# A read of shifted positions that also waits for the head two further on

## The chip, the cores and the metric

The kernel runs on one core of a Trainium2 chip. The metric is the device time of one execution in microseconds, the median of several runs.

## What is computed

The reference normalises x (32 sequences of 512 tokens, 256 wide) and adds to x an attention with relative positions and a mixture of experts. Only the attention matters here. For each of 32 x 16 heads:

```python
content_score = jnp.einsum('bhsp,bhtp->bhst', q + u, k)
pos_score = jnp.einsum('bhsp,htp->bhst', q + v, pos)
pos_score = _relative_shift(pos_score)
score = (content_score + pos_score) / jnp.sqrt(jnp.float32(P))
weights = jax.nn.softmax(score, axis=-1)
out = jnp.einsum('bhst,bhtp->bhsp', weights, val)
```

`_relative_shift` puts a zero column before a 512 x 512 matrix, reads the same memory as rows of 512, and drops the first one. It is a pure change of addresses.

## The kernel before

**Stages.** A first stage (up to about 180 us) normalises x, stores it and computes the gate. The attention follows, up to about 3,360 us, one head after the other: 16 iterations of 32 heads (two sequences). Iterations 0 to 2 and 15 are written out, iterations 3 to 14 are one hardware loop. The experts follow.

**One head through the engines.** The body of every engine counts steps `kk` of 0 to 31, and one step is one head long. Head n (counted over all iterations) goes through these places:

- TensorE computes its position scores (L978) in step n-5, in four quarters.
- ScalarE copies them out of PSUM in two halves (`x_evacuate`, L605) into `ring`, with a zero column in front. The second half ends at the end of step n-5 and brings the semaphore `x_out` to 2(n+1).
- SyncE waits for that and writes the head to memory (`write_x`, L397), 1,026 KB, into one of 8 slots of `xs_d`.
- GpSimd waits until this write has landed (`x_written`), and until the slot of `shifted` that it will fill is free (`t_full`, head n-8), and reads the head back (`read_x`, L497), 1,024 KB, one row further on. That is the relative shift. In the order of GpSimd's program the read of head n stands at the beginning of step n-3.
- VectorE adds the shifted positions to the content scores (`add`, L745), first quarter at the end of step n-1. This is the first use of what was read, and the first quarter waits for the read (`x_shifted`).
- ScalarE takes the exponential (L610), TensorE transposes (L1011), and VectorE and ScalarE copy that out (L755, L619). TensorE multiplies with the values (L1027).

Reads and writes of heads are thus long transfers of about 1 MB, on two queues: q1 (SyncE) and q0 (GpSimd).

**What else stands in GpSimd's program.** GpSimd splits operands into a high and a low part, in the order of its own program:

```python
for kk in range(BH):
    t = kk // MH + 1
    if not (last and kk + LEAD - 2 >= BH):
        read_x(i, kk + LEAD - 2)
    if kk % MH == 4 and not (last and t >= TILES):
        keys(i, t)
    if kk % MH == 5 and not (last and t >= TILES):
        with_u(i, t)
    if kk % MH == 6 and t % 2 and not last:
        split_xt(i * 2 + 2 + t // 2, t // 2)
    if kk % MH == MH - 1 and not (last and t + 1 >= TILES):
        with_v(i, t + 1)
```

Here `MH` is 8 (heads in one tile of queries), `LEAD` is 5. `with_u` and `with_v` are a CAST (L457) and a TENSOR_TENSOR (L459) each. `with_u` reads `qn[:, 0]` and `with_v` reads `qn[:, 1]`. `keys` is L477 and L479, `split_xt` is L487 and L489.

**Who waits for these.** Once in 8 heads, ScalarE writes the next tile of queries into `qn` (`keep_queries`, two ACTIVATEs, L569). It overwrites what `with_u`, `with_v` and `keys` read, so it waits for all three of the tile before (`qu_low`, `qv_low`, `k_low`). It stands in ScalarE's step `kk % 8 == 6`, behind the first two exponentials, and ahead of the first half of `x_evacuate` (L605) of that step. TensorE waits for it (`q_kept`), because the projection and `spread_kd` (L900, L902) use one PSUM bank in turn, and then goes on with the scores of the same step. The `with_u` whose result frees `qn[:, 0]` stands in GpSimd's step `kk % 8 == 5`, directly behind the read of head kk+3.

**Boundary of the loop.** At the start of each turn of the hardware loop TensorE and ScalarE pause for new instructions. Step 0 is then 12 to 17 us long instead of 5 to 7.

Of the kernel before, what the change touches and what calls it, by code (L numbers as in the profile page):

```python
# [41 lines left out]
def wait(eng, sem, value):  # L42

    if isinstance(value, int) and value <= 0:
        return
    eng.wait_ge(sem, value)


def wait_alone(eng, sem, value):

    wait(eng, sem, value)
    if not isinstance(value, int):
        eng.nop(nofuse=True)
# [92 lines left out]
def attention_phase(nc, x, gate_w, w, w1, w2, consts, xn_d, xt_d, xs_d, att_d, sums_d, shared):  # L146
# [5 lines left out]
    EARLY = 3  # L152
    LEAD = 5
    LAG = 2
    NX = 8
    NW = 4
    BH = 2 * H
# [5 lines left out]
    ITERS = B // 2  # L163
    with ExitStack() as ctx:
# [11 lines left out]
        pos = m.sb("pos", [P, NG8, S], F32R)  # L176
        shifted = m.sb("shifted", [P, NX, TT, S])

# [18 lines left out]
        xo = shared.ring[:, :].rearrange("p (k t c) -> p k t c", k=NW, t=TT)  # L197
        mn = m.sb("mn", [P, NX, TT])
        pt = m.sb("pt", [P, TT, S])
# [89 lines left out]
        x_out = m.sem("x_out")  # L289
        x_written = [m.sem(f"x_written{k}") for k in range(NX)]  # L290
        x_shifted = [m.sem(f"x_shifted{k}") for k in range(NX)]
        s_full = m.sem("s_full")
# [25 lines left out]
        def values_at(kk, last):  # L318

            half = {9: 0, H - 1: 1}.get(kk % H)  # L320
            return (kk // H + 1, half) if half is not None and not (last and kk // H + 1 >= 2) else None
# [9 lines left out]
        def of_slot(kk):  # L331

            return kk % NX, kk // NX

# [4 lines left out]
        with nc.Block() as block:  # L339

            @block.sync
            def _(sp):
# [48 lines left out]
                def write_x(i, kk):  # L391
# [3 lines left out]

                    wait_alone(sp, x_shifted[slot], (i * (BH // NX) + turn) * 16)
                    sp.dma_start(xs_d[slot].rearrange("(p t c) -> p t c", t=TT, c=S + 1), xo[:, kk % NW]).then_inc(x_written[slot], 16)  # L397
# [43 lines left out]
            def _(pool):  # L441
# [49 lines left out]
                def read_x(i, kk):  # L491

                    slot, turn = of_slot(kk)
                    wait_alone(pool, x_written[slot], (i * (BH // NX) + turn + 1) * 16)

                    wait_alone(pool, t_full, (i * BH + kk - NX + 1) * TT)
                    pool.dma_start(shifted[:, slot], xs_d[slot][S:S + S * S].rearrange("(p t c) -> p t c", t=TT, c=S)).then_inc(x_shifted[slot], 16)  # L497
# [7 lines left out]
                pool.wait_ge(p_low, DC)  # L505
                pool.wait_ge(w_low, 1)
                read_x(0, 0)
                for n in range(NS):
                    pool.wait_ge(xn_stored[n], 16 * (B // NS))
                    pool.wait_ge(xt_stored[n], 16 * (B // NS))  # L510
                read_x(0, 1)
                read_x(0, 2)
                with_v(0, 1)
                split_xt(1, 1)
# [27 lines left out]
            def _(act):  # L542
# [56 lines left out]
                def x_evacuate(i, kk, half):  # L599

                    if half == 0 and not (isinstance(i, int) and i * BH + kk < NW):
                        slot, turn = of_slot(kk - NW)
                        act.wait_ge(x_written[slot], (i * (BH // NX) + turn + 1) * 16)
                    act.wait_ge(x_full, (i * BH + kk) * 2 + half + 1)
                    act.activation(xo[:, kk % NW, 2 * half:2 * half + 2, 1:S + 1], xp[:, :, :], ACT.Copy).then_inc(x_out, 1)  # L605

                def exponential(i, kk, t):

                    act.wait_ge(added, (i * BH + kk) * TT + t + 1)
                    act.activation(shifted[:, kk % NX, t], shifted[:, kk % NX, t], ACT.Exp, bias=mn[:, kk % NX, t:t + 1],  # L610
                                   scale=-1.0).then_inc(exp_done, 1)

                def t_evacuate(i, kk):

                    n = i * BH + kk
                    act.wait_ge(t_full, (n + 1) * TT)

                    wait(act, o_full, n)
                    act.activation(pt[:, TT - 1], tp[:, 1], ACT.Copy).then_inc(t_out_act, 1)  # L619

                def o_evacuate(i, q):
                    u = i * QUADS + q
                    act.wait_ge(o_full, (u + 1) * QH)

                    wait(act, o_stored[q % 2], (u - q % 2) * (TT * 16))
                    act.activation(osb[:, q % 2].rearrange("p h t -> p (h t)"), op[:, :], ACT.Copy).then_inc(o_out, 1)
# [15 lines left out]
                def body(i):  # L642
                    first = isinstance(i, int) and i == 0
                    last = isinstance(i, int) and i == ITERS - 1
                    for kk in range(BH):
# [15 lines left out]
                        if positions:  # L661
                            x_evacuate(i, kk + LEAD, 1)
                        if not (first and kk < LAG):
                            t_evacuate(i, kk - LAG)
                        if kk % QH == 2 and not (first and kk < QH):
# [3 lines left out]
                for t in range(1, TT):  # L669
                    exponential(ITERS, -1, t)  # L670
                for k in range(LAG):
                    t_evacuate(ITERS, k - LAG)
                o_evacuate(ITERS - 1, QUADS - 1)

            @block.vector
            def _(dve):
# [61 lines left out]
                def add(i, kk, t):  # L738

                    n = i * BH + kk  # L740
                    if t == 0:
                        slot, turn = of_slot(kk)
                        wait_alone(dve, x_shifted[slot], (i * (BH // NX) + turn + 1) * 16)
                    wait_alone(dve, s_full, n * TT + t + 1)
                    dve.tensor_tensor_reduce(out=shifted[:, kk % NX, t], in0=sp_[:, t % 2], in1=shifted[:, kk % NX, t], scale=-0.25,  # L745
                                             scalar=-NEG, op0=ALU.add, op1=ALU.min,
                                             accum_out=mn[:, kk % NX, t:t + 1]).then_inc(added, 1)

                def t_evacuate(i, kk, t):
                    n = i * BH + kk  # L750
                    dve.wait_ge(t_full, n * TT + t + 1)
                    if t == 0:

                        wait(dve, o_full, n)
                    dve.tensor_copy(pt[:, t], tp[:, t % 2]).then_inc(t_out_dve, 1)  # L755
# [74 lines left out]
                def body(i):  # L830
                    first = isinstance(i, int) and i == 0
                    last = isinstance(i, int) and i == ITERS - 1
                    for kk in range(BH):
                        even, odd = even_group(kk, last), odd_group(kk, last)
                        values = values_at(kk, last)
                        turning = not (first and kk < LAG)
                        add(i, kk, 1)
                        add(i, kk, 2)
                        if turning:
                            t_evacuate(i, kk - LAG, 0)  # L840
                            t_evacuate(i, kk - LAG, 1)
# [738 lines left out]
def build(nc, x, Wq, bq, Wk, bk, Wv, bv, Wp, bp, Wo, bo, u, v, gate_w, w1, w2, out):  # L1580
    names = ("sinusoid", "ident", "first_row", "spread")
    c = {n: nc.inline_tensor(a, name=f"const_{n}").ap() for n, a in zip(names, shape_constants())}
    xn_d = nc.dram_tensor("xn_d", [B * S, D], F32).ap()
    xt_d = nc.dram_tensor("xt_d", [B, P, DC, S], F32).ap()
    ffn_d = nc.dram_tensor("ffn_d", [B * S, D], F32).ap()
    xs_d = nc.dram_tensor("xs_d", [S * P + 8 * S * (S + 1)], F32).ap()[S * P:].rearrange("(k n) -> k n", k=8)
    att_d = nc.dram_tensor("att_d", [B, D, S], F32).ap()
    sums_d = nc.dram_tensor("sums_d", [B, H, S], F32).ap()
    inv_d = nc.dram_tensor("inv_d", [B, H, S], F32).ap()
    mid_d = nc.dram_tensor("mid_d", [B, S, D], F32).ap()  # L1590
    weights = {"Wq": Wq, "Wk": Wk, "Wv": Wv, "Wp": Wp, "bq": bq, "bk": bk, "bv": bv, "bp": bp,
               "u": u.rearrange("a h b p -> (a h b p)"), "v": v.rearrange("a h b p -> (a h b p)")}
    with ExitStack() as ctx:
        shared = Shared(nc, ctx)
        attention_phase(nc, x, gate_w, weights, w1, w2, (c["sinusoid"], c["ident"], c["first_row"], c["spread"]), xn_d, xt_d, xs_d,
                        att_d, sums_d, shared)
        ffn_phase(nc, x, Wo, bo, w1, w2, xn_d, shared, ffn_d, att_d, sums_d, inv_d, mid_d, out)
# [27 lines left out]
```

## Time and profile before

| | us |
|---|---|
| median of 3 runs (range) | 5040.58 (5020.95 to 5041.53) |
| the profiled execution | 5030.14 |
| its span, first to last instruction | 5028.3 |
| TensorE busy | 4825.9 (96%) |
| VectorE busy | 3691.6 |
| ScalarE busy | 3462.9 |
| GpSimd busy | 1711.7 |
| mean granted clock of TensorE | 0.98 |

Times in the rows are microseconds from the start of the span, unless marked ns. PE is TensorE's matmul, PEld its weight load, DVE VectorE, ACT ScalarE, POOL GpSimd and SPq SyncE, which only issues transfers. L497 is a line of the kernel. A row of the timeline has start, duration, engine, line, operation, what is written and read, how many were merged, and in brackets how long the engine sat idle before it and what ended that. Where several semaphores were waited for, the bracket names the last event that the profile could find; it can name an engine that had long been done.

### The profile page before, as it was taken

Reading aid. Unit: us, or ns where it says so; the run is one execution under the profiler, and the core shown is the slowest. Engines: PE = TensorE matmul, PEld = TensorE weight load, DVE = VectorE, ACT = ScalarE, POOL = GpSimd, SP = SyncE. Lnnn points to the kernel's source line nnn. Section 1 sums busy time; section 2 is a strip of 40 time slices with the busy share of each in tenths; the row PEclk is TensorE's granted clock in tenths of the full one; section 3 lists DMA queues with packets and bytes.
Section 4 is the critical chain, followed back from the end, with each engine's and each line's share of the span. In section 5 each row is a group of like instructions: output and inputs, shape, how many; then the busy total and the mean of one; then the engine's idle time right before and its main releaser. Section 6 shows DMA issues by size and latency. Waiting matters only on the chain. (4 is left out here: it accounts for less than half of the span.)

```text
span 5028.3 us, 126515 instructions
## 1 busy us (share of the span) xinstructions
PE 4825.9 (96%) x42412; PEld 3683.7 (73%) x42412; DVE 3691.6 (73%) x8040; ACT 3462.9 (69%) x5180; POOL 1711.7 (34%) x1545
## 2 busy tenths in 40 slices
PE   7899999999999999999999999989999999999997
PEld 3566666676676666766666667758999898998997
DVE  7799998898898888988888889874455545444344
ACT  3688888898888888988978889864433333344454
POOL 1122222232223222322222222224566565544443
PEclk9899999999999999999999999999999999999999
DMA  9899999999999999999999999986445455433359
GB/s 351 318 361 347 332 360 342 351 361 337 366 349 345 362 335 346 366 343 359 359 328 360 339 344 366 366 296 179 100 115 141 113 133 140 109 62 68 60 146 312
DMA packets 320461, 1391.16 MB, mean 277 GB/s; under 512 B 42912, under 2 KB 120608, under 8 KB 188448
## 3 DMA queue, kind: packets, MB, share of 16 engines
q1 hardware_dynamic: 196896, 778.35, 41.7%
q0 software_dynamic: 122880, 604.05, 39.3%
q8 instruction: 385, 6.31, 0.5%
q14 instruction: 300, 2.46, 0.1%
HBM read 708.00 MB, written 674.23 MB: 275 GB/s over the span
## 5 line engine op out<-in xcount | busy, mean ns | idle before, releaser
L745 DVE CUSTOM_DVE_ANT_0 att_shifted<-att_quad,att_shifted 128x512 f32<-128x512 f32 x2048 | 1327.1, 684 | 213.2 <-PE att_quad L990 170.5
L610 ACT ACTIVATE att_shifted<-att_shifted,att_mn 128x512 f32<-128x512 f32 x2048 | 1361.9, 717 | 122.0 <-issue 100.4
L605 ACT ACTIVATE ring<-att_quad 128x1024 f32<-128x1024 f32 x1024 | 1047.1, 1023 | 310.8 <-PE att_quad L978 309.5
L1011 PE MATMUL att_tp<-ident,att_shifted 128*128 128x128 f32 x8192 | 1134.4, 282 | 7.1 <-issue 4.4
L755 DVE COPY att_pt<-att_tp 128x512 f32<-128x512 f32 x1536 | 1011.8, 686 | 141.2 <-PE att_tp L1011 124.0
L1011 PEld LDWEIGHTS att_tp<-ident,att_shifted 128*128 128x128 f32 x8192 | 886.8, 142 | 308.3 <-issue 145.4
L497 POOL DMA_DIRECT2D att_shifted<-xs_d x512 | 279.3, 545 | 2249.7 <-DMA xs_d<-ring 1259.3
L1482 DVE TENSOR_TENSOR ffn_hp<-ring,ffn_hp 128x512 fp32r<-128x512 f32 x512 | 474.6, 927 | 683.8 <-ACT ring L1419 638.3
L1417 ACT ACTIVATE ffn_hp<-ffn_up 128x512 fp32r<-128x512 f32 x512 | 306.0, 598 | 920.5 <-PE ffn_up L1563 864.8
L978 PE MATMUL att_quad<-att_pos,att_qv 64*128 64x512 f32 x2048 | 848.1, 454 | 38.3 <-ACT ring L605 38.2
L990 PE MATMUL att_quad<-att_kd,att_qu 64*128 64x512 f32 x2048 | 787.0, 456 | 68.9 <-issue 50.0
L1524 PE MATMUL ffn_yp<-ffn_w2p,ffn_hp 128*128 128x256 f32 x6144 | 827.7, 284 | 4.0 <-DVE ffn_hp L1482 2.3
L1524 PEld LDWEIGHTS ffn_yp<-ffn_w2p,ffn_hp 128*128 128x128 f32 x6144 | 798.7, 191 | 41.7 <-DVE ffn_hp L1482 2.7
L1563 PE MATMUL ffn_up<-ffn_xp,ffn_w1p 128*128 128x512 f32 x3072 | 795.8, 394 | 6.7 <-DVE ffn_xp L1442 2.8
L1357 POOL DMA_INDIRECT ffn_d<-ring,picks x256 | 431.1, 1684 | 702.2 <-DVE ring L1450 688.9
L990 PEld LDWEIGHTS att_quad<-att_kd,att_qu 64*128 64x128 f32 x2048 | 318.9, 187 | 438.4 <-issue 304.8
L1563 PEld LDWEIGHTS ffn_up<-ffn_xp,ffn_w1p 128*128 128x128 f32 x3072 | 546.4, 190 | 98.1 <-issue 4.5
L1027 PE MATMUL att_op<-att_pt,att_val 128*17 128x128 f32 x16384 | 559.3, 278 | 7.1 <-issue 0.2
L1027 PEld LDWEIGHTS att_op<-att_pt,att_val 128*17 128x17 f32 x16384 | 409.7, 98 | 199.5 <-issue 149.9
L978 PEld LDWEIGHTS att_quad<-att_pos,att_qv 64*128 64x128 f32 x2048 | 351.6, 188 | 71.3 <-ACT ring L605 41.4
L619 ACT ACTIVATE att_pt<-att_tp 128x512 f32<-128x512 f32 x512 | 306.2, 598 | 30.3 <-PE att_tp L1011 27.6
L1419 ACT ACTIVATE ring<-ffn_up 128x512 f32<-128x512 f32 x512 | 303.9, 593 | 8.1 <-DVE ffn_hp L1482 7.5
(111 smaller groups left out, 4707.7 us busy)
## 6 DMA issues: line engine op xcount, KB each, us to landing
xs_d<-ring SPq DMA_DIRECT2D x512, 1026.0 KB, 9.4
att_shifted<-xs_d POOLq DMA_DIRECT2D x512, 1024.0 KB, 9.9
att_shifted<-in_L_attn_x_dram SPq DMA_DIRECT2D x32, 512.0 KB, 7.2
xn_d<-att_shifted SPq DMA_DIRECT2D x32, 512.0 KB, 6.5
xt_d<-att_shifted SPq DMA_DIRECT2D x32, 512.0 KB, 7.6
gathered<-xt_d SPq DMA_DIRECT2D x32, 512.0 KB, 11.6
att_d<-att_osb SPq DMA_DIRECT2D x512, 32.0 KB
ring<-in_L_ffn_w_dram SPq DMA_DIRECT2D x16, 1024.0 KB
```

What stands on the lines that cost most here:

```text
L605: act.activation(xo[:, kk % NW, 2 * half:2 * half + 2, 1:S + 1], xp[:, :, :], ACT.Copy).then_inc(x_out, 1)
L610: act.activation(shifted[:, kk % NX, t], shifted[:, kk % NX, t], ACT.Exp, bias=mn[:, kk % NX, t:t + 1], scale=-1.0).then_inc(exp_done, 1)
L745: dve.tensor_tensor_reduce(out=shifted[:, kk % NX, t], in0=sp_[:, t % 2], in1=shifted[:, kk % NX, t], scale=-0.25, scalar=-NEG, op0=ALU.ad ...
L755: dve.tensor_copy(pt[:, t], tp[:, t % 2]).then_inc(t_out_dve, 1)
L978: ins = pe.matmul(xp[:, t % 2, :], qv[rows, kk // GH % 2, t * P:(t + 1) * P], pos[rows, kk // GH % NG8, :], start=True, stop=True)
L990: pe.matmul(sp_[:, t % 2, :], qu[rows, kk // GH % 2, t * P:(t + 1) * P], kd[rows, kk // GH % 2, :], start=True, stop=True).then_inc(s_full, 1)
L1011: ins = pe.transpose(tp[:, c % 2, t * P:(t + 1) * P], shifted[:, kk % NX, t, c * P:(c + 1) * P], ident[:, :])
L1027: ins = pe.matmul(op[32 * t:32 * t + HD + 1, kk % QH * P:(kk % QH + 1) * P], val[:, kk // H % 2, c, kk % H, :], pt[:, c, t * P:(t + 1) * P ...
L1357: pool.indirect_dma_start(ffn_d, bass.IndirectOffsetOnAxis(ap=picks[:, g * GB + k, e:e + 1], axis=0), ys[:, g % 2, k], None, compute_op=AL ...
L1482: dve.tensor_tensor(hp[:, g % 2, 1, f], hf[:, f % 2], hp[:, g % 2, 0, f].bitcast(F32), ALU.subtract).then_inc(h_low, 1)
L1524: ins = pe.matmul(yp[:, k % 2, 0:D], hp[:, g % 2, hi, f, k * CAP:(k + 1) * CAP], w2p[:, wi, f, :], start=(f == 0 and s == 0), stop=(f == F ...
L1563: ins = pe.matmul(up[:, f % 4, :], w1p[:, wi, c, f * P:(f + 1) * P], xp[:, g % 2, xi, c, :], start=(s == 0 and c == 0), stop=(s == 2 and c ...
```

## The change

`read_x` on GpSimd gets one more wait. Beside its own write's landing, the read of head n waits until `x_out` shows that head n+2 has been copied out of PSUM. This is the very count for which SyncE waits before it issues the write of head n+2. In the last iteration the head waited for is capped at the last one.

```diff
     LAG = 2
+    BESIDE = 2
     NX = 8
...
                     wait_alone(pool, x_written[slot], (i * (BH // NX) + turn + 1) * 16)
+                    final = isinstance(i, int) and i == ITERS - 1
+                    with_write = min(kk + BESIDE, BH - 1) if final else kk + BESIDE
+                    wait_alone(pool, x_out, (i * BH + with_write + 1) * 2)
 
                     wait_alone(pool, t_full, (i * BH + kk - NX + 1) * TT)
```

`wait_alone` is a wait, and behind it a nop of its own where the value is a register's (in the hardware loop). No transfer and no computation is added or removed.

## Rows read from the trace of the kernel before

**Rows 1.** The page: busy time of each engine over the span.
```profile
PE 4825.9 (96%) x42412; PEld 3683.7 (73%) x42412; DVE 3691.6 (73%) x8040; ACT 3462.9 (69%) x5180; POOL 1711.7 (34%) x1545
```

**Rows 2.** Stretches: from:to, length, busy of the engines, clock, DMA share, GB/s.
```profile
1400.00:1800.00 400.00, 383.38 (x3949) 269.52 (x3950) 340.77 (x805) 340.58 (x487) 106.88 (x120) 0.97 0.97 349
...
1783.00:1799.00 16.00, 16.00 (x133) 10.93 (x134) 11.68 (x28) 12.34 (x19) 0.53 (x1) 0.80 0.58 229
...
1862.00:1869.00 7.00, 7.00 (x69) 5.03 (x69) 5.56 (x14) 6.48 (x10) 2.83 (x3) 1.00 0.99 390
```

**Rows 3.** Timeline, step 14 of one loop turn: with_u done early.
```profile
1861.02 0.57 POOL L497 DMA_DIRECT2D att_shifted<-xs_d  x1 [1.37 <-PE att_tp L1011]
...
1862.18 1.02 ACT L605 ACTIVATE ring<-att_quad 128x1024 f32<-128x1024 f32 x1 [0.56 <-PE att_quad L978]
...
1862.80 0.69 DVE L745 CUSTOM_DVE_ANT_0 att_shifted<-att_quad,att_shifted 128x512 f32<-128x512 f32 x1
1862.86 1.55 POOL L459 TENSOR_TENSOR att_qc<-att_qn,att_qc 128x512 fp32r<-128x512 f32 x1
...
1863.33 6.79 SPq L397 DMA_DIRECT2D xs_d<-ring  x2
...
1864.92 1.25 ACT L569 ACTIVATE att_qn<-att_mp,att_bias_q 128x512 f32<-128x512 f32 x2
...
1867.00 0.48 PE L900 MATMUL att_mp<-att_kc,att_spread 128*128 128x512 f32 x1
...
1869.26 0.69 DVE L745 CUSTOM_DVE_ANT_0 att_shifted<-att_quad,att_shifted 128x512 f32<-128x512 f32 x1
...
1874.91 0.69 DVE L745 CUSTOM_DVE_ANT_0 att_shifted<-att_quad,att_shifted 128x512 f32<-128x512 f32 x1
```

**Rows 4.** Timeline, step 22 of a later turn: with_u done late.
```profile
2705.30 1.02 ACT L605 ACTIVATE ring<-att_quad 128x1024 f32<-128x1024 f32 x1 [0.56 <-PE att_quad L978]
...
2705.91 0.69 DVE L745 CUSTOM_DVE_ANT_0 att_shifted<-att_quad,att_shifted 128x512 f32<-128x512 f32 x1
2706.10 0.57 POOL L497 DMA_DIRECT2D att_shifted<-xs_d  x1 [4.54 <-PE att_tp L1011]
...
2707.92 1.56 POOL L459 TENSOR_TENSOR att_qc<-att_qn,att_qc 128x512 fp32r<-128x512 f32 x1
...
2709.56 1.26 ACT L569 ACTIVATE att_qn<-att_mp,att_bias_q 128x512 f32<-128x512 f32 x2 [1.42 <-issue]
...
2710.88 0.50 PE L900 MATMUL att_mp<-att_kc,att_spread 128*128 128x512 f32 x1 [0.51 <-ACT att_qn L569]
...
2712.96 0.69 DVE L745 CUSTOM_DVE_ANT_0 att_shifted<-att_quad,att_shifted 128x512 f32<-128x512 f32 x1
...
2719.06 0.69 DVE L745 CUSTOM_DVE_ANT_0 att_shifted<-att_quad,att_shifted 128x512 f32<-128x512 f32 x1
```

**Rows 5.** L569 (keep_queries): its count, and what its engine idled for before.
```profile
L569 ACT ACTIVATE att_qn<-att_mp,att_bias_q x128: 672/681/692, 107.6 to 3251.0; 128x512 f32<-128x512 f32 x128
...
  issue: 16.0, 24
```

**Rows 6.** Issues of the two transfers: count, KB, median us to landing.
```profile
xs_d<-ring SPq DMA_DIRECT2D x512, 1026.0 KB, 9.4
att_shifted<-xs_d POOLq DMA_DIRECT2D x512, 1024.0 KB, 9.9
```

**Rows 7.** Waits over the span: who for whom, us in total, times, longest.
```profile
POOL att_shifted L497 <- DMA xs_d<-ring: 1259.3, 268, 31.9
...
DVE att_shifted L745 <- DMA att_shifted<-xs_d: 24.8, 23, 2.8
```

**Rows 8.** Timeline: TensorE's first matmul after the pause at a loop turn.
```profile
1775.01 0.79 PE L990 MATMUL att_quad<-att_kd,att_qu 64*128 64x512 f32 x1 [4.79 <-issue]
```

**Rows 9.** Timeline: copy-out of head 278, first add of head 276.
```profile
1886.34 1.02 ACT L605 ACTIVATE ring<-att_quad 128x1024 f32<-128x1024 f32 x1 [0.56 <-PE att_quad L978]
...
1897.88 0.69 DVE L745 CUSTOM_DVE_ANT_0 att_shifted<-att_quad,att_shifted 128x512 f32<-128x512 f32 x1
```

## The prediction

> **What bounds the kernel now.** I read the page first. TensorE is busy for 96% of the span [rows 1], and in a plain stretch of the attention for 383 of 400 us [rows 2]. So whatever makes TensorE wait in the attention is paid, and little else is. In the same stretch the DMA engines show a share of 0.97 and 349 GB/s, and 390 GB/s in a dense seven microseconds [rows 2]. They are close to a limit too. The list of waits then tells how often the transfers decide: VectorE waited only 24.8 us, 23 times, for a shifted head [rows 7]. The reads have slack at nearly every head.
>
> Then I went to the timeline, for two questions. When is the read of head n issued now, against the copy-out of head n+2? And what stands behind it on GpSimd? In the ordinary case the copy-out of the second half (L605) ends at 1862.18 + 1.02 = 1863.20 and the read had been issued at 1861.02, 2.18 us earlier [rows 3]. It follows its own write's landing [rows 7], and a write takes 9.4 us while two steps take 11 to 13 [rows 6, 3]. So in most steps the new wait ends last, and the read moves later.
>
> **Part 1, the direct one: the read comes later.** Nothing is added to the transfers. The read is now issued at the end of the copy-out of head n+2 plus some 0.2 us. SyncE, which waits for the same count, issued at 1863.33, 0.13 us behind the end [rows 3]; GpSimd has one more wait and a nop to pass, so I take 0.2 (0.1 to 0.4 as bounds). What is left until its first use? The shortest case [rows 9]: the copy-out of head 278 ends at 1887.36 and the first add of head 276 starts at 1897.88, which is 10.52 us. With 0.2 for the issue and about as much again for the wake of VectorE, the read must land within about 10.1 us. Its median is 9.9 [rows 6]. In the timeline 6 of 32 steps have a window this short; the others have 11.6 us or more. Six heads in 16 iterations are 96 reads, half of them over the median. If these are late by 0.5 us on average, that is 24 us of new waits.
>
> Against it stands the 24.8 us of old waits [rows 7]. They occur when the DMA engines are behind, at 390 GB/s. Part 2 below lengthens every eighth step by 1.5 us, 3% of some 50 us, so the same bytes ask for about 339 GB/s instead of 349. I expect over half of the old waits to go, and not all of the 24 to come. I set this part at 0, with bounds of -25 (all old waits gone, no new ones) and +40 (new waits with little relief).
>
> On this the Trainium skill has a rule that speaks against the change: "DMA: Bandwidth & Descriptors", section "Rules for kernel authors", says to issue a DMA early and wait for it late. By that rule alone every read loses what it is delayed by; the trace agrees only where the slack is smaller than the delay, and that is the 0 to 40 us above.
>
> At the start of a loop turn the delay is much larger. There TensorE pauses for instructions [rows 8], and the reads of the next two heads are issued during the pause; now they wait for a copy-out that comes only behind it. But in the 16 us after the pause the DMA share is 0.58 [rows 2], so a late read finds free engines. I cost it at nothing. What covers it is that idle share; without it these two reads would have the 10.5 us window as well. The instruction loads of the pause might meet less traffic, a gain. The pause shown is 4.79 us; if half of it were contention, 13 turns would give at most 30 us. No row shows the split, so I take 0 and keep -30 for the range.
>
> **Part 2, the one that I expect to decide: what is queued behind the read on GpSimd.** The engine works in order. Behind the read of step `kk % 8 == 5` stands `with_u`. ScalarE's `keep_queries` in the next step may not overwrite `qn` before `with_u` is done. And the count that now releases this read is ScalarE's own last copy-out of step 5, after which ScalarE needs only a short time until it comes to `keep_queries`.
>
> - How soon ScalarE comes: in the ordinary case L569 starts at 1864.92, 1.72 us behind the end of the copy-out at 1863.20 [rows 3].
> - How long GpSimd needs from the issue of the read to the release: in the late case the read is issued at 2706.10, the second part of `with_u` ends at 2707.92 + 1.56 = 2709.48, and L569 starts at 2709.56. That is 3.46 us [rows 4].
> - So behind the change L569 starts 0.2 + 3.46 = 3.66 us after the copy-out, 1.94 us later than when nothing holds it.
>
> What does such a lateness cost? The trace has the experiment in it. In the late case the read happened to be issued only 0.22 us ahead of the end of the copy-out (2706.32), and L569 started 3.24 us behind that end, 1.52 us late. TensorE then idled before L900, with L569 as releaser [rows 4]. The two steps around it, from add to add, took 2719.06 - 2705.91 = 13.15 us, against 1874.91 - 1862.80 = 12.11 us in the ordinary case [rows 3, 4]. So 1.52 us late cost 1.04, and 0.48 are hidden. At 1.94 us late the cost is 1.46 us.
>
> How often? L569 has 128 instructions, two for a tile, so 64 tiles [rows 5]. The first two are made before the steady order begins; 62 remain. 62 x 1.46 = 90.5 us. Part of this is paid already: ScalarE idled 16.0 us, 24 times, before L569 [rows 5]. Taking 0.48 hidden off each gives 4.5 us, too little, since short ones cost nothing rather than less than nothing; 16 is the upper bound. I take 7. The net is **+83 us**. Bounds: at 1.04 us each 64 us, less 16, is 48; at 0.4 us for the issue it is 103, less 4.5, is 98.
>
> The other pieces on GpSimd have cover. `keys` is started up to 6 us later, behind the read of step 4, and is needed by TensorE only in the middle of step 6; the cover is one step and a half. `with_v` and `split_xt` are needed two steps and more later. GpSimd is busy 107 of 400 us [rows 2]. SyncE's writes need the reads of eight heads before, long landed.
>
> **The sum.** 83 + 0 + 0 on the profiled execution's 5030.1 us is 5113. That execution lies 10 us below the median shown and inside the range of the runs; I set 5118 between 5113 and 5040.6 + 83 = 5124.
>
> **The rivals.**
> - *Faster: the pairing relieves the transfers.* Place: the waits of VectorE for a read and the pause at a loop turn. If read and write in one rhythm make the old waits vanish (-25) and the instruction loads quicker (-30), and `with_u` cost nothing, the time would be 4975 to 5030. It decides only if `with_u` costs below 0.6 us a tile ((55 - 25 + 7) / 62) instead of 1.46. For it: the DMA share of 0.97. Against it: only 24.8 us are there to win, and the 1.04 us of rows 4 was measured. Chance 0.03 for a gain over 0.5%.
> - *No change:* `with_u` late but hidden, or paid back by fewer waits for reads: 5020 to 5060. For it: ScalarE idles before L605 in each step, 0.56 us in rows 3. Against it: that is contained in the 0.48 hidden. Chance 0.05.
> - *Much slower: the read becomes the bound.* If writes and reads issued at one moment take longer each, say 11 us instead of 9.9, a read is late by 0.9 us in the six short windows and just in time in the others: 96 x 0.9 = 86 us on top, about 5200. For it: two transfers of 1 MB start together with engines already at 390 GB/s. Against it: since about 1.6 of each kind are in flight at any time already (9.9 us against steps near 6 us), they overlap now as well. Chance 0.10.
> - *The change does nothing,* because the write always lands last. Rows 3 exclude it. It is contained in "no change".
>
> The Trainium skill bears on the third rival: "DMA: Bandwidth & Descriptors", section "Queues, rings and completion order", says that a DMA engine takes packets in turn from the queues that have work. By it, transfers of two queues started together share the engines and both end late; the trace has them overlapping throughout, so no run of before shows it apart.
>
> **How the numbers follow.** The forecast (part 2 in full, reads about even) has 0.82 and is 5118. From 48 to 98 us for part 2, and -25 to +40 for the reads, the range is 5075 to 5155; it leaves out the no-change case, the far rival and a little of the rest. A measurement of this kernel cannot tell under 0.5% from no change, 25 us here. Slower by over 0.5%: 0.82 + 0.10 = 0.92. Within 0.5%: 0.05. Faster: 0.03.
>
> **What the profile after would show.** L569 preceded by idle time of ScalarE at nearly every tile, near 1.5 to 2 us, 90 to 120 us in total against 16. TensorE idle before L900 with L569 as releaser, some 0.8 us and more, once in eight heads. L497 within 0.1 to 0.4 us of the end of L605 in most steps. VectorE's wait for reads between 10 and 60 us. The number of instructions is unchanged but for waits. The prediction is wrong if L569's idle time stays near 16 us; if it grows and the steps around it do not; or if VectorE's wait for reads grows past 80 us.

## The result and the profile after

The changed kernel takes 5178.71 us (median of 4 runs, 5173.36 to 5185.36), the kernel before 5030.76 us (median of 4, 5013.74 to 5041.53). The ratio is 1.0298, with a 95% interval from 1.026 to 1.0336. That is slower, as forecast, but by about 148 us where 83 were worked out, and above the range. The profiled execution took 5175.65 us, with a span of 5173.8.

First the page of the changed kernel, busy time of each engine and the two transfers (count, KB, median us to landing). Line numbers after the change are 4 higher from L497 on (read_x is L501, x_evacuate L609, keep_queries L573, add L749, spread_kd L904).

```profile
PE 4893.4 (95%) x42412; PEld 3724.2 (72%) x42412; DVE 3707.6 (72%) x8040; ACT 3470.3 (67%) x5180; POOL 1714.4 (33%) x1545
...
xs_d<-ring SPq DMA_DIRECT2D x512, 1026.0 KB, 8.9
att_shifted<-xs_d POOLq DMA_DIRECT2D x512, 1024.0 KB, 9.2
```

A plain stretch of the attention, in the columns of [rows 2]:

```profile
1400.00:1800.00 400.00, 371.62 (x3749) 260.40 (x3751) 324.00 (x763) 323.63 (x463) 102.57 (x116) 0.97 0.93 330
```

Look at three things. The same number of instructions took TensorE 67 us longer than in [rows 1]: it did not only wait, in part it also ran slower, at a mean granted clock of 0.976 against 0.980. The median transfer lands sooner than in [rows 6], reads in 9.2 us against 9.9. And the engines for transfers are less loaded, 0.93 against 0.97, 330 GB/s against 349. The kernel is not slower because transfers as a whole got slower.

Now the waits (who for whom, us in total, times, longest):

```profile
POOL att_shifted L501 <- ACT ring L609: 1945.1, 412, 37.6
...
ACT att_qn L573 <- issue: 140.7, 62, 2.3
...
PEld att_mp L904 <- ACT att_qn L573: 98.3, 62, 1.7
...
PE att_mp L904 <- ACT att_qn L573: 83.5, 62, 1.4
...
DVE att_shifted L749 <- DMA att_shifted<-xs_d: 72.1, 64, 3.8
```

The first line says that the new wait ends last at most reads. The next ones are the chain of the prediction: ScalarE idle before `keep_queries` 62 times for 140.7 us, against 24 times and 16.0 us in [rows 5], and TensorE idle behind it 62 times. The last is the wait for reads, 72.1 us against the 24.8 of [rows 7].

One of the 62 places in the timeline, to be set beside [rows 3] and [rows 4]:

```profile
1891.46 1.03 ACT L609 ACTIVATE ring<-att_quad 128x1024 f32<-128x1024 f32 x1 [0.56 <-PE att_quad L982]
...
1892.08 0.69 DVE L749 CUSTOM_DVE_ANT_0 att_shifted<-att_quad,att_shifted 128x512 f32<-128x512 f32 x1
...
1892.62 8.78 SPq L398 DMA_DIRECT2D xs_d<-ring  x2
...
1893.15 0.57 POOL L501 DMA_DIRECT2D att_shifted<-xs_d  x1 [2.96 <-ACT ring L609]
...
1895.01 1.54 POOL L460 TENSOR_TENSOR att_qc<-att_qn,att_qc 128x512 fp32r<-128x512 f32 x1
...
1896.63 1.27 ACT L573 ACTIVATE att_qn<-att_mp,att_bias_q 128x512 f32<-128x512 f32 x2 [2.31 <-issue]
...
1897.95 0.50 PE L904 MATMUL att_mp<-att_kc,att_spread 128*128 128x512 f32 x1 [1.42 <-ACT att_qn L573]
...
1900.03 0.69 DVE L749 CUSTOM_DVE_ANT_0 att_shifted<-att_quad,att_shifted 128x512 f32<-128x512 f32 x1
1900.62 0.48 PE L904 MATMUL att_mp<-att_qc,att_spread 128*128 128x512 f32 x1
```

The copy-out ends at 1891.46 + 1.03 = 1892.49 and the read is issued at 1893.15, which is 0.66 us later, not the 0.2 of the sum (SyncE, released by the same count, issues at 1892.62, 0.13 us later). `keep_queries` starts 4.14 us behind the copy-out, where 3.66 were forecast and 1.72 is what it needs. The first step, add to add, takes 1900.03 - 1892.08 = 7.95 us.

At 24 of the 62 places there is more. Here is one, from the second step on:

```profile
3143.43 0.50 PE L904 MATMUL att_mp<-att_kc,att_spread 128*128 128x512 f32 x1 [1.41 <-ACT att_qn L573]
...
3145.53 1.97 PE L1015 MATMUL att_tp<-ident,att_shifted 128*128 128x128 f32 x8
3147.15 0.77 PE L904 MATMUL att_mp<-att_qc,att_spread 128*128 128x512 f32 x1
...
3149.94 1.10 PE L1015 MATMUL att_tp<-ident,att_shifted 128*128 128x128 f32 x8
```

And the two places as stretches (the columns are those of [rows 2]; look at the sixth value after the length, the granted clock):

```profile
1900.00:1906.00 6.00, 5.95 (x65) 4.17 (x64) 5.51 (x14) 5.82 (x10) 4.01 (x3) 1.00 0.97 362
...
3145.00:3149.00 4.00, 4.00 (x20) 2.46 (x22) 2.50 (x7) 3.00 (x5) 1.62 (x2) 0.59 0.89 371
```

TensorE had idled 1.41 us before L904 in one case and 1.42 in the other. In the second its clock then fell to the lower of its two levels, 1.2 GHz, for 3.4 us: eight transposes took 1.97 us instead of 1.10, a 512-column matmul 0.77 instead of 0.48. In the other case it stayed at 2.4 GHz. I counted such stretches in the granted clock of the whole attention, its last steps left out: 25 outside the first two steps of an iteration, none in the kernel before. In the 50 places of iterations 3 to 15, the two steps took 15.38 us on average in the 20 cases with such a stretch and 13.94 us in the 30 cases without; before they took 12.11 undisturbed. There is nothing in between: the 30 reach 14.1 us at most, the 20 start at 15.2. So a fall of the clock goes with 1.4 us.

Where the span's 145.5 us are, by the first adds of the heads:

| place | us |
|---|---|
| steps 6 and 7 of each tile, 62 x (14.38 - 12.20) | +135 |
| - of it low clock, 24 x 1.4 | 34 |
| - of it the lateness at full clock | 101 |
| first two steps of a loop turn, 12 x (19.88 - 21.29) | -17 |
| all the rest | +27 |

The loop turns counted are those of iterations 3 to 14, where TensorE and VectorE are in their hardware loop. GpSimd, ScalarE and SyncE loop over iterations 1 to 14 (`ends_apart`), so iteration 2 has long first steps too; it is in the rest. The waits for reads grew by 47 us; how far the rest follows them is worked out below from the other profiles.

### The profile page after: what moved, and what is told of

It is laid out like the page before. It is cut to its first block and busy times, and to the rows that moved or that the text cites. A ratio compares the mean times of both kernels' runs of the same rounds, so it can differ in the third digit from the quotient of the medians.

```text
span 5173.8 us, 127419 instructions
## 1 busy us (share of the span) xinstructions
PE 4893.4 (95%) x42412; PEld 3724.2 (72%) x42412; DVE 3707.6 (72%) x8040; ACT 3470.3 (67%) x5180; POOL 1714.4 (33%) x1545
## 5 line engine op out<-in xcount | busy, mean ns | idle before, releaser
L749 DVE CUSTOM_DVE_ANT_0 att_shifted<-att_quad,att_shifted 128x512 f32<-128x512 f32 x2048 | 1333.9, 686 | 233.2 <-PE att_quad L994 92.5
L609 ACT ACTIVATE ring<-att_quad 128x1024 f32<-128x1024 f32 x1024 | 1048.7, 1024 | 324.5 <-PE att_quad L982 323.2
L1015 PE MATMUL att_tp<-ident,att_shifted 128*128 128x128 f32 x8192 | 1157.7, 286 | 6.8 <-DVE att_pt L759 6.2
L1015 PEld LDWEIGHTS att_tp<-ident,att_shifted 128*128 128x128 f32 x8192 | 905.3, 144 | 309.4 <-issue 161.1
L501 POOL DMA_DIRECT2D att_shifted<-xs_d x512 | 280.4, 548 | 2475.4 <-ACT ring L609 1945.1
L982 PE MATMUL att_quad<-att_pos,att_qv 64*128 64x512 f32 x2048 | 861.9, 458 | 31.4 <-ACT ring L609 31.4
L994 PE MATMUL att_quad<-att_kd,att_qu 64*128 64x512 f32 x2048 | 808.2, 460 | 69.4 <-issue 38.5
## 6 DMA issues: line engine op xcount, KB each, us to landing
gathered<-xt_d SPq DMA_DIRECT2D x32, 512.0 KB, 10.8
```

Of the source, the lines that this page charges most:

```text
L982: ins = pe.matmul(xp[:, t % 2, :], qv[rows, kk // GH % 2, t * P:(t + 1) * P], pos[rows, kk // GH % NG8, :], start=True, stop=True)
L994: pe.matmul(sp_[:, t % 2, :], qu[rows, kk // GH % 2, t * P:(t + 1) * P], kd[rows, kk // GH % 2, :], start=True, stop=True).then_inc(s_full, 1)
L1015: ins = pe.transpose(tp[:, c % 2, t * P:(t + 1) * P], shifted[:, kk % NX, t, c * P:(c + 1) * P], ident[:, :])
```

## The experiments

Each is compared with the kernel before on the same chip.

**1. with_u ahead of the read.**

```diff
+                        if kk % MH == 5 and not (last and t >= TILES):
+                            with_u(i, t)
                         if not (last and kk + LEAD - 2 >= BH):
                             read_x(i, kk + LEAD - 2)
...
-                        if kk % MH == 5 and not (last and t >= TILES):
-                            with_u(i, t)
```

> The changed kernel, with with_u put ahead of the read in GpSimd's step kk % 8 == 5; every read keeps its new wait. If with_u behind the read is the cause of most of the loss (copy-out to L573 2.3 us late, 62 times, and TensorE's low clock behind the idle time), ScalarE's idle time before L573 falls from 141 us to under 20, the extra low-clock stretches go, and the time is 0 to 30 us above before. If the later reads are the cause (rival: a read paired with a write is slower, or its window too short), VectorE's wait for reads stays at 70 us or grows, and the time stays above before by 80 us or more.

Measured: 5060.86 us against 5025.12, ratio 1.0077 (1.0048 to 1.0106). Three quarters of the loss are gone with one call moved, with all reads as late as before. Its waits:

```profile
DVE att_shifted L749 <- DMA att_shifted<-xs_d: 90.9, 84, 3.3
...
ACT att_qn L573 <- issue: 1.3, 1, 1.3
```

ScalarE's idle time before `keep_queries` went from 140.7 us to 1.3, and low-clock stretches outside the loop starts from 25 to 3. So what stands behind the read decides. But the 36 us that stay are above the 30 that I allowed, and the waits for reads grew to 90.9 us. The profile shows where: 30 us of these waits are at the reads of heads with n % 8 == 0, which had 0.8 us in the changed kernel. Their median read took 11.5 us in iterations 3 to 14, against 9.8. These waits fall around steps 6 and 7, which are still 38 us longer than before. In the changed kernel the late `keep_queries` gives these reads a window of 13.6 us or more; here it is about 12. So the lateness of `keep_queries` had been their cover.

**2. and 3. The wait at one read in eight, and at the other seven.**

```diff
+                    if kk % MH == 0:
+                        wait_alone(pool, x_out, (i * BH + with_write + 1) * 2)
-                    wait_alone(pool, x_out, (i * BH + with_write + 1) * 2)
```

and the same with `!= 0`.

> The new wait only for heads with n % 8 == 0, the read behind which with_u stands. If with_u is the cause: L573 late at 62 places as in the changed kernel, 110 to 145 us slower than before, with VectorE's wait for reads near 25 us or less. If the later reads in general are the cause: one read in eight is delayed, under 30 us slower.

> The new wait for all heads but n % 8 == 0, with nothing moved. With_u theory: ScalarE's idle time before L573 stays near 16 us; time within 0 to 30 us above before, as in the run with with_u ahead. Later-reads theory: 80 us or more above before. Sum of this run's and the one-in-eight run's excess should be near the changed kernel's 148 us if the two parts add up.

Measured: 5112.16 us for the one in eight, ratio 1.018 (1.0149 to 1.0212), and 5033.06 for the seven, ratio 1.0011 (0.9993 to 1.0028). By the ratios, the one read in eight costs 90 us, the other seven about 5, within what cannot be told from nothing. The verdict for `with_u` is clear, yet 90 is less than the 110 to 145 expected, and 90 + 5 is not 148. The profile of the one in eight shows where it went:

```profile
ACT att_qn L574 <- issue: 140.9, 62, 2.3
...
DVE att_shifted L750 <- DMA att_shifted<-xs_d: 4.8, 3, 2.8
```

ScalarE's idle time is that of the changed kernel. Steps 6 and 7 take 14.52 us, 144 us more than before over the 62 tiles. But the waits for reads fell from 24.8 us to 4.8, and the first two steps of a loop turn from 21.29 to 17.12 us, 50 us over 12 turns. The profile of the seven in eight has the other half:

```profile
DVE att_shifted L750 <- DMA att_shifted<-xs_d: 65.4, 64, 3.6
```

Here ScalarE idles only 5.6 us before `keep_queries`, and the waits for reads are nearly those of the changed kernel. Side by side, as differences from the profile before, in us (one profile each; that of the seven in eight is the slowest of its ten executions, 5044.5):

| | steps 6 and 7 | first two steps of a loop turn | rest of the attention | VectorE's waits for reads, in all |
|---|---|---|---|---|
| before | 0 | 0 | 0 | 24.8 |
| one in eight | +143 | -50 | -12 | 4.8 |
| seven in eight | -3 | -16 | +30 | 65.4 |
| all (the changed kernel) | +135 | -17 | +28 | 72.1 |

The +28 is of the attention; over the whole span it is the +27 above.

The first column is the one read with `with_u` behind it, and the rest of the attention follows the waits for reads. The two experiments add up to the changed kernel in both of these columns within some 10 us. In the loop turns they do not: -66 against -17. That is the interaction of some 50 us between the two parts. With one read in eight held, the other reads of a loop turn are issued early and the turn is short; with all held, most of this relief is lost. Why is not shown.

**4. The wait without its delay.** `BESIDE = 1` instead of 2.

> BESIDE = 1: the read of head n waits for the copy-out of head n+1, which ends some 5.5 us earlier and nearly always before the write has landed. It prices the wait as an instruction, with no delay. Both theories: within 10 us of before, L573 as in before. If the wait itself (instructions on GpSimd) mattered, some 0.1 us more from landing to read and a loss of up to 20 us.

Measured: 5024.13 us against 5026.79, ratio 1.0 (0.9987 to 1.0012). The time from a write's landing to the issue of its read went from 0.65 to 0.78 us in the loop, the 0.1 us that the expectation had, and it costs nothing that can be told in the whole: it is when the wait ends that counts.

**5. TensorE kept at work (twice).** In step `kk % 8 == 6` four transposes are made three times into the same bank. Nothing is left out.

```diff
-                    for t in range(TT):
-                        ins = pe.transpose(tp[:, c % 2, ...
+                    for again in range(3 if c == 1 and (kk + LAG) % MH == 6 else 1):
+                        for t in range(TT):
+                            ins = pe.transpose(tp[:, c % 2, ...
```

> The changed kernel, where TensorE repeats the four transposes of the second turn in step kk % 8 == 6 twice more (8 extra, about 1.1 us) into the same PSUM bank ahead of its idle 1.4 us before L904. The results are the same. If the low clock behind that idle time costs some 1.4 us at 20 to 25 of 62 places (theory), the low-clock stretches in steps 6 and 7 vanish, the second step is 6.1 us instead of 7.5 at all of them, and the time falls by 25 to 40 us against the changed kernel. If the 7.5 us steps have another cause (transfers), nothing changes, or the extra work makes it slower.

> The changed kernel with repeated transposes again, with a second profile. In the first, steps 6 and 7 were 33 us shorter over 62 tiles but the loop turns 29 us longer (22.3 against 19.9 and 19.6 us in two profiles of the changed kernel). If the longer turns belong to the longer program, they repeat at 21.5 or more; if they were chance, they come back to 20 and the time falls to 25 to 35 us below the changed kernel.

Measured: 5171.34 us, ratio 1.0298 (1.0269 to 1.0328); again 5161.8, ratio 1.0303 (1.0279 to 1.0328). Beside the changed kernel's 1.0298, and 1.0277 when it was measured again, that is no gain; the fall of 25 to 40 us did not come. The first profile:

```profile
ACT att_qn L573 <- issue: 141.3, 62, 2.3
...
PE att_mp L904 <- ACT att_qn L573: 29.4, 58, 0.6
```

`keep_queries` is as late as in the changed kernel, but TensorE idles 0.6 us at most ahead of L904, and no low-clock stretch falls into these steps (0 of 62 in both profiles, against 24, and 27 in a second profile of the changed kernel). The two steps take 13.85 us on average instead of 14.38, which is 33 us over 62 tiles, just the 24 x 1.4. So the low clock is shown to be the cause of the 15.4 us cases. The time did not fall because the first two steps of a loop turn took 22.28 and 22.45 us instead of 19.88, 29 us over 12 turns. It repeated, so it belongs to this kernel. The queue that carries instructions shows why (packets, MB, share of the DMA engines), first in the changed kernel, then here:

```profile
q8 instruction: 385, 6.31, 0.5%
...
q8 instruction: 397, 6.50, 0.5%
```

That is twelve packets of 16 KB more, eleven of them in iterations 3 to 14, and the same again in the second profile. And TensorE stops a second time in a turn:

```profile
2047.33 0.79 PE L994 MATMUL att_quad<-att_kd,att_qu 64*128 64x512 f32 x1 [4.30 <-issue]
...
2052.95 1.48 PE L1032 MATMUL att_op<-att_pt,att_val 128*17 128x128 f32 x22 [3.22 <-issue]
```

The changed kernel has one stop of over 2.5 us at each of the 12 turns, this one has two at 11 of them, in both profiles. So the longer program asks for more instructions at each turn, and its second stop fits that; that the stop waits for just these packets is argued.

**6. The changed kernel again.**

> The changed kernel once more, for a second profile and as the partner of the run with repeated transposes. Step 0 and 1 at the 12 loop turns differed from kernel to kernel by up to 5 us a turn (17.1 to 22.3 us). If that is chance, this second profile differs from the first by a few us a turn too; if it is fixed by the kernel, it repeats at 19.9 within 0.5. Low-clock stretches outside the loop start again 20 to 30.

Measured: 5172.04 us, ratio 1.0277 (1.0255 to 1.0298). The second profile has 140.7 us before `keep_queries` again, 66.8 us of waits for reads, 27 low-clock places, and 19.58 us at the loop turns (19.88 in the first). What a kernel shows at its loop turns, on average over the 12, repeats within some tenths of a microsecond, here and in the fifth experiment.

**7. The small stores moved.** SyncE issues the eight small stores of four heads' output in step `kk % 4 == 2` instead of 0.

```diff
-                        if kk % QH == 0 and not (first and kk < 2 * QH):
+                        if kk % QH == 2 and not (first and kk < 2 * QH):
                             store_o(i, kk // QH - 2)
```

> The changed kernel with the eight small stores of a group's output issued by SyncE in step kk % 4 == 2 instead of 0. In the changed kernel the reads of heads with n % 8 == 4 take 11.4 to 12.3 us, those of the others 8 to 10.7, and VectorE waits for them at a window of 10.4 us. If the small stores, queued ahead of the transfers, make these reads long, then the long reads move to other heads (n % 4 == 2 or 3), whose window is 11.6 us, and VectorE's wait for reads falls from 72 us to under 30, the time by 15 to 30 us. If it is only the sequence of short steps, the long reads stay at n % 8 == 4 and the time stays.

A read that is late in the changed kernel, head 268 (268 % 8 is 4). The copy-out of head 270 ends at 1917.37, the read is issued at 1918.03 and VectorE stands still until 1930.54, 13.17 us behind the copy-out. The third line is the time to landing of this one read, the last that of the read issued at 1901.62 (head 265):

```profile
1916.34 1.03 ACT L609 ACTIVATE ring<-att_quad 128x1024 f32<-128x1024 f32 x1 [0.55 <-PE att_quad L982]
1918.03 0.53 POOL L501 DMA_DIRECT2D att_shifted<-xs_d  x1 [4.97 <-ACT ring L609]
...
DMA to landing us min/median/max: 11.9/11.9/11.9
...
1930.54 0.69 DVE L749 CUSTOM_DVE_ANT_0 att_shifted<-att_quad,att_shifted 128x512 f32<-128x512 f32 x1 [1.36 <-DMA att_shifted<-xs_d]
...
DMA to landing us min/median/max: 8.3/8.3/8.3
```

Measured: 5160.5 us, ratio 1.0262 (1.0241 to 1.0282), 11.5 us under the changed kernel in the same comparison, less than the 15 to 30 expected, and the two intervals overlap. Its profile:

```profile
DVE att_shifted L749 <- DMA att_shifted<-xs_d: 31.9, 37, 2.6
```

The waits for reads fell by 40 us, and the long reads moved. With the stores in their old place the median read of heads 12, 20 and 28 took 11.6, 11.4 and 12.3 us, with the stores moved 9.7, 9.2 and 9.5; heads 6, 22 and 30 now take 10.8 to 11.6. So the small stores make the read beside them long. The window that it misses, from the copy-out to the first add without the wait, is 10.6 us for head 20 and 11.8 for heads 12 and 28, counted within an iteration. The other windows of 10.4 to 10.5 us, for reads of 8 to 9 us, have hardly a wait. The waits fell by 40 us and the time by some 12. The profile splits that: outside steps 6 and 7 and the loop turns the attention is 16 us shorter, the loop turns are 6 us shorter, but steps 6 and 7 are 10 us longer, with 30 low-clock places instead of 24. So a part of the gain went to the low clock, and of 40 us of waits some 16 count.

**8. The kernel before with with_u ahead.** Moved as in the first experiment, without the new wait.

> The kernel before with with_u ahead of the read in step kk % 8 == 5. Before, L569 was held 24 times by with_u, at a price I put at 7 us. Theory: the idle time before L569 falls under 5 us, time 0 to 10 us below before. Rival (a read issued up to 3 us later behind with_u costs as much): time equal or up to 15 us above.

Measured: 5023.38 us against 5026.79, ratio 0.999 (0.9979 to 1.0001). The idle time before `keep_queries` is gone, and steps 6 and 7 take 12.11 us on average instead of 12.20, 5.6 us over 62 tiles. That is near the 7 us that I had taken as already paid. The waits for reads rose from 24.8 to 35.8 us, though, and in the time the gain is at the edge of what can be told.

**9. Both moves, in the changed kernel and in the one before.**

> The changed kernel with with_u ahead of the read and the small stores two steps later. If the loss had only these two parts, the time is within 10 us of before (with_u ahead alone left 36 us, most of it put down to waits for reads), and VectorE's wait for reads falls from 91 to under 40 us. If the loss left is of another kind, it stays 25 us or more above before.

> The kernel before with both: with_u ahead of the read, and the small stores two steps later. Theory: VectorE's wait for reads falls from 25 us to under 15, and with with_u's part it is 5 to 25 us faster than before. Rival: the stores only move the late reads, time within 5 us of before.

Measured: the changed kernel with both takes 5045.36 us against 5012.25, ratio 1.0067 (1.0042 to 1.0091). It stays 33 us above before, with 68.7 us of waits for reads. The stores do not explain the rest. The waits moved with them: from heads with n % 8 == 4 (51 of 72 us in the changed kernel, 1 here) to n % 8 == 1, 6 and 7 (17 to 18 us each). The kernel before with both takes 5008.5 us against 5012.25, ratio 0.9982 (0.9967 to 0.9998), the lowest ratio of all; that is 4 us by the medians and 9 by the ratio. Its waits for reads:

```profile
DVE att_shifted L745 <- DMA att_shifted<-xs_d: 18.7, 16, 2.8
```

against 24.8 before. It is the only version whose interval lies below 1, and only just: a gain of some 0.2%, at the edge of what can be told.

How much the waits for reads weigh can now be read from the profiles together. The rest of the attention, as its difference from before, is -12 us at 4.8 us of waits, -5 at 18.7, 0 at 24.8, +12 at 31.9, +9 at 35.8, +19 at 56.2, 58.3 and 66.8, +30 at 65.4, +23 at 68.7 and +28 at 72.1. With `with_u` ahead it is +26 at 90.9, and there a third of the waits is in steps 6 and 7, which are not in this rest. So the +27 of the changed kernel go with the waits for reads, in most profiles at about half to three quarters of a microsecond for each microsecond of wait. No run changes these waits alone, so this is a relation and no proof.

## Why the prediction was wrong

**What was right.** That the kernel gets slower, the place, and the mechanism of the main part. The read is released late, `with_u` behind it, `keep_queries` behind that, TensorE behind that, 62 times. The first experiment takes this chain away and three quarters of the loss go with it. The slope held too. At full clock, a lateness of 4.14 - 1.72 = 2.42 us cost 13.94 - 12.11 = 1.83 us; with 0.48 us hidden, as the prediction put it, it would be 1.94.

**"GpSimd has one more wait and a nop to pass, so I take 0.2 (0.1 to 0.4 as bounds)"** is the first step that failed. It was 0.66 us at 85% of the reads of the loop, and 0.52 in iterations 0 and 15, whose waits are constants without a nop: both above the upper bound. I had carried SyncE's 0.13 over to another engine. Nearly the same, 0.65 us, lies between a write's landing and the read's issue in the trace of before, so it could have been read off. It is worth about 0.46 x 62 = 28.5 us.

**The clock was no term of the sum at all.** I had carried the cost of one late case over to all tiles. In that case TensorE idled 0.51 us before L900 [rows 4] and kept its full clock; in the changed kernel it idles 1.4. At 24 places the clock then fell, 34 us. Experiment 5 shows this as the cause.

**"I expect over half of the old waits to go, and not all of the 24 to come"** failed by its sign. Waits for reads rose from 24.8 to 72.1 us, and the rest of the span grew by 27 us. The relief was real, as the one in eight shows (4.8 us), but it needs reads that may start early, and those are what the change holds back. I had treated the two parts as independent. I had also looked at the median of all reads, against the windows of 10.5 us. The waits came where a read was long instead, 11.4 to 12.3 us beside the small stores, and two of the three such places have the 11.8 us that I had counted as safe.

**The loop start** gained 17 us, inside the bound of 30; taken as 0.

**The range** was also narrower than its own bounds: 5030 + 98 + 40 is 5168, and it ended at 5155. Of the signs that I had named, three missed in size, all the same way: 140.7 us before `keep_queries` (90 to 120), the read 0.66 us behind the copy-out (0.1 to 0.4), 72.1 us of waits for reads (10 to 60).

The sum with what was measured: 83 + 28 + 34 + 27 - 17 = 155, against 145.5. The difference is mostly the slope, which came out lower than the prediction had it, 1.83 against 1.94 us and less in the first iterations.

**The rivals.** "The read becomes the bound" comes nearest in time, 5200 against 5179, and is wrong in its mechanism. It asked for reads of 11 us everywhere; their median fell to 9.2. Reads of over 11 us came only at the heads beside the small stores, and the new waits for reads cost some 27 us, not 86. "Faster" was refuted as a whole, but both of its terms were there: with one read in eight held, the old waits and 50 us at the loop turns went. Its error was to expect them where all reads are held. "No change" fell with the steps at 14.4 us.

## What to carry to other kernels

Before a wait is put in front of an instruction, list what stands behind it on the same engine, and move the urgent part ahead; here one call moved was worth some 110 us. The time from a semaphore to an issue is to be read for the engine in question, from a wait that it has already. And a new idle stretch of TensorE can have two prices, at full clock and at the lower one, here 1.8 and 3.3 us for the same lateness. One example from the trace that kept its full clock gives only the first.

## What was unexpected of the hardware

- GpSimd issues its transfer 0.66 us after the end of the ScalarE instruction that releases it, SyncE 0.13 us. The Trainium skill, "DMA: Bandwidth & Descriptors", section "Anatomy of one DMA — SWDGE (gpsimd) path", gives about 50 ns for the sequencer's dispatch, and calls the making of the descriptors small, as parts of the time of one DMA. It gives no time from a semaphore to the issue. That time is thirteen times the 50 ns in this kernel, with a further wait and nops in it, so the dispatch cannot stand in for it; the measured 0.66 decides.
- An idle time of TensorE of 1.4 us was followed by 3.4 us at 1.2 GHz in 24 and 27 of 62 cases (two profiles), and by none in the others; what decides between them is not shown. With 0.6 us at most it was 0 of 62, twice. A fall cost 1.4 us.
- Eight small stores (four of 32 KB, four of 2 KB) made the 1 MB read beside them take 11.4 to 12.3 us instead of 9.2 to 9.7, at three of the four heads of an iteration with n % 8 == 4.
- The first two steps of a loop turn took between 17.1 us (one read in eight held) and 22.4 us (longer program), repeatable for a kernel. TensorE's stops of over 1 us in them add up to 3.1 and 7.0 us a turn in these two, to 4.2 in the changed kernel and 5.7 before, in these four in the order of the turns' lengths. What sets the stops of the same program stays open.
